# Two chained cross-attentions and their feed-forwards: new orders on every engine, and the last two batches' second-attention stacks kept in the first attention's buffers

## What is computed

```python
x = x + xattn0(layernorm(x), ctx, ctx)      # 16 heads of 16, 128 queries x 128 keys, causal mask
x = x + ffn0(layernorm(x), ...)             # base matrix + 8 LoRA experts, two picked by a router
x = x + gamma * xattn1(layernorm(x), ctx)   # 8 heads of 16 rows, 256 queries x 256 keys (rows are channels), no mask
x = x + ffn1(x, ...)                        # RMS norm, 8-bit quantised 256->1024, GELU, quantised 1024->256
```

## Time and profile before

| | us |
|---|---|
| median of 3 runs | 407.16 (403.74 to 408.58) |
| the profiled execution | 404.29 |
| its span, first to last instruction | 402.6 |
| outside the span | 1.7 |
| busy: PE / DVE / POOL / ACT | 306.0 / 315.4 / 268.4 / 262.1 |
| mean share of full TensorE clock | 0.919 |

### The profile page before, as it was taken

The page is one execution under the profiler, slowest core; times in us unless marked ns, Lnnn a source line. Parts: engine busy times, 40 slices in busy tenths (PEclk is TensorE's granted clock), DMA queues, the critical chain, the costliest instruction groups (busy, mean ns, idle before and its releaser), DMA issues.

```text
span 402.6 us, 9610 instructions
## 1 busy us (share of the span) xinstructions
PE 306.0 (76%) x2946; PEld 189.5 (47%) x2946; DVE 315.4 (78%) x841; ACT 262.1 (65%) x501; POOL 268.4 (67%) x508
## 2 busy tenths in 40 slices
PE   0156757568889999999987999999768777556784
PEld 0134544435646556556564575665334333334553
DVE  6734447399899688799995998998786467999993
ACT  2313435425769699698686786687455348989993
POOL 5554798777988888979996795655621113677554
PEclk9988667587899999999999999999897689999999
DMA  5677578675686775756775756623451400001111
GB/s 182 184 236 241 136 176 227 164 200 166 164 222 152 210 221 153 220 174 178 219 188 157 221 154 195 133 71 77 95 119 38 95 1 2 0 15 40 42 54 65
DMA packets 73138, 56.21 MB, mean 140 GB/s; under 512 B 5376, under 2 KB 62592, under 8 KB 73088
## 3 DMA queue, kind: packets, MB, share of 16 engines
q1 hardware_dynamic: 69888, 51.67, 47.1%
q10 hardware_dynamic: 3200, 3.93, 3.5%
HBM read 36.45 MB, written 18.87 MB: 137 GB/s over the span
## 4 chain that ended last, share of the span: by engine, by line
PE 24%; DVE 19%; issue 19%; POOL 13%; DMA 13%; SPq 6%; ACT 4%; POOLq 0%; ACTq 0%; DVEq 0%
DMA q<-max_t 7%; DVE max L1833 6%; DMA k_parts<-k_split 4%; PE ps_u L1226 4%; PE ps_st L1195 3%; DVE hq_t L2293 2%; PE ps_s L1180 2%; PE ps_st L1166 2%; SPq L622 2%; PE ps_ff L1296 2%; PE ps_s L1146 2%; SPq L623 2%; POOL p L904 2%; PE ps_s L1150 1%; PE ps_t L1324 1%
## 5 line engine op out<-in xcount | busy, mean ns | idle before, releaser
L1833 DVE TENSOR_REDUCE max<-ps_s 128x2 f32<-128x512 f32 (+1 forms) x192 | 126.9, 680 | 38.5 <-PE ps_s L1180 21.5
L1547 ACT ACTIVATE p<-ps_st 128x512 f32<-128x512 f32 x128 | 71.1, 599 | 20.2 <-PE ps_st L1195 13.7
L1180 PE MATMUL ps_s<-k,q 96*128 96x256 bf16 x256 | 52.0, 288 | 7.5 <-issue 3.2
L904 POOL TENSOR_SCALAR_AFFINE_SELECT p<-p 128x512 f32<-128x512 f32 x64 | 40.0, 637 | 16.6 <-ACT p L1537 16.4
L1195 PE MATMUL ps_st<-q,k 98*128 98x256 bf16 x256 | 47.3, 286 | 3.8 <-ACT p L1547 2.1
L1537 ACT ACTIVATE p<-ps_st 128x512 f32<-128x512 f32 x64 | 35.6, 600 | 21.1 <-PE ps_st L1166 20.7
L1226 PE MATMUL ps_u<-p,v 128*32 128x256 f32 x512 | 39.9, 425 | 6.0 <-POOL v L894 3.6
L1166 PE MATMUL ps_st<-q,k 98*128 98x128 bf16 x256 | 27.1, 250 | 16.8 <-DMA q<-max_t 16.2
L1180 PEld LDWEIGHTS ps_s<-k,q 96*128 96x128 bf16 x256 | 19.4, 100 | 27.3 <-issue 14.2
L1195 PEld LDWEIGHTS ps_st<-q,k 98*128 98x128 bf16 x256 | 21.4, 100 | 20.9 <-issue 7.1
L1166 PEld LDWEIGHTS ps_st<-q,k 98*128 98x128 bf16 x256 | 21.2, 113 | 21.3 <-DMA q<-max_t 13.9
(11 more groups left out here) (144 smaller groups left out, 793.4 us busy)
## 6 DMA issues: line engine op xcount, KB each, us to landing
k_parts<-k_split SPq DMA_DIRECT2D x16, 512.0 KB, 3.8
q<-q_parts SPq DMA_DIRECT2D x32, 256.0 KB, 4.1
k<-k_parts SPq DMA_DIRECT2D x32, 256.0 KB, 3.7
kv_in<-in_kv SPq DMA_DIRECT2D x16, 256.0 KB, 3.8
q_parts<-q_t SPq DMA_DIRECT2D x16, 256.0 KB, 3.7
q<-q_parts SPq DMA_DIRECT2D x32, 128.0 KB, 4.0
k<-k_parts SPq DMA_DIRECT2D x32, 128.0 KB, 3.6
q_parts<-q_split SPq DMA_DIRECT2D x16, 256.0 KB, 2.0
```

The lines of the kernel that those rows point to most:

```text
L904: pool.affine_select(out=kept, in_=kept, compare_op=ALU.is_ge, fill=0.0, base=0, pattern=[[0, G], [1, P]], channel_multiplier=-1).then_inc ...
L1180: last = pe.matmul(out_[:, f * D:(f + 1) * D], q1[0:STK, odd, h * D + f * P:h * D + (f + 1) * P], k1[0:STK, odd, h * D:(h + 1) * D], start ...
L1547: act.activation(p1[:, h, :], ps_st[bank_of(ST_BANKS, f"s1t{h}")][:, :], ACT.Exp, scale=SCALE).then_inc(exp1_done[h], 1)
L1833: dve.tensor_reduce(out_, src, AX.X, ALU.max, negate=True).then_inc(done, 1)
```

## The change

Four parts. (1) The orders of `fill` and `drain` are written anew on every engine, those of `body` on SP, POOL, DVE and in two places on PE (`pv0` of unit 3 goes before unit 0, `pv1(1, 1)` before the last `scores1_t`). (2) In passes 19 and 20 the loads of batches 14 and 15 for the second attention go into `k0` and `q0`, whose last first-attention use is over in pass 17 or 18; they wait for that instead of for batches 12 and 13. (3) `load_v1` has stage 7 instead of 6, `dequant_in` 20 instead of 19. (4) `copy_hid`, `down`, `scale_output`, `add_output` and the store move one stage back, and the program has one pass more. No operation is added or left out.

```diff
-LOAD_V1 = 6
+LOAD_V1 = 7
-DEQUANT_IN = 19
+DEQUANT_IN = 20
-COPY_HID = 27
-DOWN = 28
+COPY_HID = 28
+DOWN = 29
...
-MAX1_UNITS = MAX1, ((6, 5, 2, 0, 1, 3, 7, 4), (5, 6, 2, 0, 1, 3, 7, 4), (5, 6, 2, 0, 1, 3, 7, 4))
+MAX1_UNITS = MAX1, ((5, 6, 2, 0, 1, 3, 7, 4), (5, 6, 2, 0, 1, 3, 7, 4), (5, 6, 2, 0, 1, 3, 7, 4))
...
+def among_last(b, n):
+
+    return isinstance(b, int) and b >= NB - n
...
+        def stacks1(b):
+
+            return (k0, q0) if among_last(b, 2) else (k1, q1)
...
-                if later(b, 2):
+                if among_last(b, 2):
+                    sp.wait_ge(st0_ready[in_turn(S0T_UNITS, b)[-1]], b + 1)
+                    plain(sp)
+                elif later(b, 2):
                     sp.wait_ge(st1_ready[in_turn(S1T_UNITS, b, 2)[-1]], free)
                     plain(sp)
                 sp.wait_ge(k_parts_out, stored_)
                 plain(sp)
-                load_stack(sp, k1, odd, k_parts[b, 1], K_SECOND, k1_landed)
+                load_stack(sp, stacks1(b)[0], odd, k_parts[b, 1], K_SECOND, k1_landed)
...
             def body(t, odd):
                 load_kv(t, odd)
+                store_k(t)
                 rows1(t, odd)
-                store_k(t)
-                load_q0(t, odd)
                 rows0(t, odd)
+                load_v1(t, odd)
                 load_k0(t, odd)
+                load_q0(t, odd)
                 store_q1(t)
-                load_v1(t, odd)
                 load_k1(t, odd)
                 load_q1(t, odd)
                 store_q0(t)
```

More of the change, by code:

```diff
@@ L772, in body @@
                 load_kv(t, odd)
+                store_k(t)
                 rows1(t, odd)
-                store_k(t)
+                rows0(t, odd)
+                load_v1(t, odd)
+                load_k0(t, odd)
                 load_q0(t, odd)
-                rows0(t, odd)
-                load_k0(t, odd)
                 store_q1(t)
-                load_v1(t, odd)
                 load_k1(t, odd)
@@ L784, in drain @@
             def drain(t, odd):
+                load_kv(t, odd)
                 store_k(t)
+                store_q0(t)
                 rows1(t, odd)
+                load_q0(t, odd)
+                load_v1(t, odd)
+                rows0(t, odd)
                 load_k0(t, odd)
-                rows0(t, odd)
-                store_q0(t)
                 store_q1(t)
-                load_kv(t, odd)
-                load_q0(t, odd)
                 load_k1(t, odd)
                 load_q1(t, odd)
-                load_v1(t, odd)
                 store_out(t)
@@ L997, in fill @@
             def fill(t, odd):
+                if t == 2:
+                    rstd0_group(2)
+                q1_mid(t)
                 k_rest_(t, odd)
-                q1_mid(t)
+                q1_low(t)
+                k_mid(t)
                 place_v0(t, odd)
@@ L1339, in fill @@
                 scores1_t(t, odd, 4)
+                scores1_t(t, odd, 6)
+                scores1_t(t, odd, 2)
+                turn_u0(t)
                 scores1(t, odd, 6)
-                turn_u0(t)
                 scores1(t, odd, 0)
                 scores1(t, odd, 2)
+                turn_gated(t)
+                scores1_t(t, odd, 1)
+                turn_back(t)
+                scores0_t(t, odd, 2)
                 scores0_t(t, odd, 1)
-                turn_gated(t)
-                scores1_t(t, odd, 2)
+                pv1(t, 1, 1)
                 scores1(t, odd, 1)
                 pv1(t, 0, 1)
-                scores0_t(t, odd, 2)
-                scores1_t(t, odd, 3)
+                turn_q0(t)
                 scores1(t, odd, 3)
-                pv1(t, 0, 0)
-                turn_q0(t)
+                scores0_t(t, odd, 3)
                 scores1(t, odd, 7)
+                turn_u1(t)
+                lora(t)
                 scores1(t, odd, 4)
                 scores0_t(t, odd, 0)
-                scores0_t(t, odd, 3)
-                scores1_t(t, odd, 0)
-                lora(t)
+                pv1(t, 0, 0)
                 scores0(t, odd, 2)
+                scores0(t, odd, 3)
                 turn_max1(t)
-                scores0(t, odd, 3)
+                pv0(t, odd, 2)
                 turn_xh1(t)
@@ L1423, in body @@
                 scores1_t(t, odd, 5)
-                pv1(t, 1, 1)
             def turn_in(t):
@@ L2123, in fill @@
                 maxima1(t, 7)
-                maxima1(t, 4)
+                if t == 2:
+                    stats0_group(3)
                 if t == 4:
                     stats0_group(4)
+                maxima1(t, 4)
                 split_max1(t)
@@ L2295, in drain @@
             def drain(t, odd):
+                stats3_(t)
+                copy_hid(t)
                 logits_(t)
                 top_(t)
-                stats3_(t)
                 index(t)
-                quant_in(t)
                 gap_(t)
```

255 lines of the change are left out of this document (125 added, 130 removed).

## The result

The changed kernel takes 401.05 us, the median of nine runs (397.99 to 408.75); the kernel before, beside it, 406.67 us. The ratio is 0.9899, 95% interval 0.9856 to 0.9942: 1.0% faster, where 2.4% was forecast. Run once more beside other kernels, unaltered, it gave 0.9832 (0.9773 to 0.9892). The intervals overlap; still, ratios of different sets of runs should be compared to no better than some 0.7 points. The profiled execution took 401.05 us, its span 399.2.

What follows compares the result with a forecast made beforehand. Hand-overs and DRAM transfers bound the fill, busy engines the body. Gains of 6.4 fill, 0 body, 2.1 drain, 0 tail sum to 8.5, giving 395.8 us, median put at 397.2; forecast's own range 391 to 403, whole range 390 to 407.

Steps and rivals of the forecast that it cites:

- the store ahead costs nothing: Body: issuing the K store before the second attention's rows counted at 0; ends 3 us gained, 5 lost.
- The second rival: Body: K store delays the rows PE awaits, 2.2 us in each of eight passes, 17 us, total 413; chance 0.16.
- Start, 1.4: Fill start: first k stack load runs under the q store, so scores begin 1.4 us earlier; ends 0 and 1.4.
- Rows ahead of the loads, 2.9 net: Fill, passes 4 to 6: maxima rows issued earlier save 5.8 us of PE waits, half counted, 2.9; ends 0 and 12.0.
- first rival: Fill: bytes bound it, so the wait moves to the stacks; row terms 0, pass 7 half; median 401.7 us; chance 0.25.
- Statistics out of pass 7, 2.1: Fill, pass 7: moving six statistics on DVE behind the last maxima gains 2.1 us; ends 0 and 2.5.
- Fill together, 6.4: Fill: sum of the start, rows and statistics terms, 1.4 + 2.9 + 2.1 = 6.4 us gained.
- Drain, 2.1: Drain: 2.8 gained, 2.5 lost, 1.8 gained, sum 2.1 us; ends 4.6 gained and 0.7 lost.
- The stacks: Drain: loading batches 14 and 15 into buffers already free removes PE's waits of 1.11 and 1.73 us, 2.8 gained.
- `place_v1` behind `rms_`: Drain, passes 20 to 22: POOL places v later, 0.8 us a pass, together 2.5 us lost.
- The 1.8 us for unit 6's scores: Drain: unit 6's scores before two `pv1` let DVE finish one maximum early, 0.6 in three passes, 1.8 gained.
- Tail, 0 (±1): Tail: one pass more but no instruction more, DVE's 55.5 us stay; counted 0, ends 1 us either way.

Runs made afterwards that it cites:

- e15: Kernel before, with one pair swapped in SP's body queue: K store ahead of the rows of the second attention's maxima; 1.3% slower (5.5 us).
- e9: Changed kernel with one pair swapped back in SP's body queue: rows of the second attention's maxima ahead of the K store; ratio 0.9861.
- e14: Changed kernel with rows of the second attention's maxima ahead of the K store in SP's body queue, and v placed before the drain's small MLP steps; ratio 0.9698.
- e5: Changed kernel with SP's queue in the fill in the order of before; fill 2.0 us longer than the mean of the new ones, total time not given.
- e13: Changed kernel run once more, unaltered, beside other kernels; ratio 0.9832.
- e6: Changed kernel with the fill's last six statistics again ahead of pass 7's first maxima on DVE; pass 7 took 17.0 us, total time not given.
- e11: Kernel before with only the last two batches' second-attention stacks moved into the first attention's k and q; ratio 0.9904.
- e16: Kernel before with only the new fill and the moved stacks of the last two batches; body, drain and tail in the old orders; ratio 0.9739.
- e7: Changed kernel with the last two batches' second-attention stacks back in k1 and q1; 1.3% more time, drain 3.0 us longer than the mean of its relatives.
- e10: Changed kernel with POOL's placing of v ahead of the three small MLP steps in the drain, as before; ratio 0.9887.
- e12: New fill, drain and stacks with the body of before on all engines, and v placed ahead of the small steps in the drain; ratio 0.9799.
- e8: Changed kernel with the hidden copy, down product, scaling and output addition at their old stages, one pass less; ratio a point above 0.9899.
- e1: Changed kernel with the nine body passes in the order of before on every engine; ratio 0.9889.
- e4: Changed kernel with fill and body in the order of before, only drain orders, tail stages and last two batches' stacks new; measured time not given.

## Why the prediction was wrong in size

**The step that failed is the body's term, "the store ahead costs nothing".** It was read from the nearest row, pass 16 in the earlier trace rows, and that row was not near. The store and the rows go out together there, 0.45 us apart, as in every pass of e15. `k_low` is not the difference: it ends 1.0 us before the split in pass 16 and 1.1 before it in e15's pass 15, where PE waits 1.57 us. But batch 16 doesn't exist, so no 256 KB kv load stands ahead of the two, and PE is in the order of `drain`; which of these made the row mislead was not tried. (The row called pass 10 beside it is of pass 11 by the count of the stages.) The second rival named the mechanism rightly, its point of decision not, since pass 16 meets it without a wait, and it priced it at 2.2 us a pass, 17 in all. Alone it costs 1.3 a pass, 12 us in the profile (e15). Within the changed kernel's new orders less is left, 148.2 - 143.8 = 4.4 us (its mean body against that of e9 and e14), of which 1.9 lie in the unsteady pass 15. The ends, 3 gained and 5 lost, held; the value inside them was wrong. Against the old orders the body lost 148.2 - 144.9 = 3.3.

**Start, 1.4: right.** The turn of pass 2 stands at 23.6 instead of 25.0, and the first scores begin at 18.76, where 18.8 was forecast.

**Rows ahead of the loads, 2.9 net: half of it came.** 11.2 of the 12.0 us of waits went, twice what I counted, and 6 to 8.5 us of new ones came at the q stack, in pass 3 too, which I had not looked at: that pass grew by 2.6 us or more, from 10.8 to 13.4. Passes 3 to 6 together take 58.2 us in the mean of the four old fills and 56.8 in that of the twelve new ones, some 1.5 less. So the first rival was half right. The Trainium skill's rule that the DMA engines alternate between queue rows ("DMA: Bandwidth & Descriptors", "Queues, rings and completion order") would have kept pass 6's wait of 5.36 if the weights in ACT's queue were its cause. The wait is gone in the changed kernel, but that settles nothing: in e5, with the old queue, it is 1.23 us although the rows took 4.3 and 5.8 us to land, nearly as before (5.2 and 6.6), since PE comes to them later, behind 2.98 us for `u`. With the rows first they took 4.1 and 4.6 in the changed kernel and 1.7 and 2.0 in e13, the same code. What part the weights have in this stays open.

**Statistics out of pass 7, 2.1: too much.** Pass 7 is 1.2 us shorter in the mean, 17.4 to 16.2, and with the statistics back in their place it is 17.0 (e6): 0.8 us. The first rival had half of the term. PE waits for the gated products instead, 1.80 us.

**Fill together, 6.4.** By profiles 4.2 (100.8 - 96.6). By times 1.65 points, some 6.7 us, from e11 to e16; but these are of different sets, and their median times differ by 3.6 us only (401.05 and 397.45). The times don't decide.

**Drain, 2.1: right as a sum, by two errors.** The stacks are worth 4.8 in two passes and not 2.8 (e11; 3.0 within the changed kernel, e7), because of the clock. `place_v1` behind `rms_` costs some 2.3, near the 2.5 that was forecast: 61.6 to 59.2 (e10) and 59.5 (e14). That is luck: PE's waits only changed their names, and the gain was a pass at full clock. The 1.8 us for unit 6's scores were not seen: with v placed first, the new drain takes what the old one takes with the stacks, 59.5 (in e12 61.2). That place was not tried alone.

**Tail, 0 (±1): wrong, 2.0 lost.** Two stretches of the last 60.2 us, before and after (columns as above):

```profile
342.30:350.30 8.00, 3.80 (x31) 2.32 (x32) 7.89 (x26) 7.77 (x14) 5.62 (x16) 1.00 0.00 0
...
366.30:370.30 4.00, 2.81 (x28) 1.80 (x25) 3.96 (x11) 3.81 (x8) 2.97 (x9) 1.00 0.10 35
```

```profile
338.90:347.20 8.30, 6.93 (x35) 3.72 (x36) 8.23 (x25) 7.60 (x13) 5.43 (x14) 0.59 0.00 0
...
363.20:367.20 4.00, 4.00 (x23) 2.51 (x23) 3.14 (x9) 2.74 (x6) 2.96 (x7) 0.60 0.04 14
```

PE is busy 6.93 us for 35 records where it was 3.80 for 31: at a granted 0.59 it works most of that time at 1.2 GHz. Every kernel with the new drain shows such stretches, and so do e11 and e16 with the old one; the three tails at a mean clock of 0.98 take 77.3 to 77.4 us, those at 0.91 to 0.93 take 78.0 to 78.5, the others up to 80.2. In the pass behind the last split PE waits 1.85 us for v, where it was 1.02, but e9, which waits as long there, has a tail of 78.1. DVE is busy 55.1 of the last 64.5 us, so that the slower PE costs little. With the old stages the second stretch is absent and nothing is gained (e8); it is absent with the new stages too in e9, e10 and e14. What makes the clock fall there is not shown. The forecast's 0 took for granted that the tail would stay at its clock of 1.00.

**The sum.** By the parts of the profiles, in means, 4.2 - 3.3 + 2.7 - 2.1 = 1.5 us were gained where 8.5 were forecast: the body lacks 3.3 of it, the fill 2.2 and the tail 2.1, and the drain gave 0.6 more. In times the new fill and the stacks have 2.6 points (e16), about as much as the whole forecast, and the changed kernel in the same set has 1.7: the new orders of body, drain and tail give back 0.9. So the gain was there, and a loss beside it that I had seen and set at nothing. The profiles give less than the times; the profiled execution of before lies 2.4 us below its median, and that difference is not located.

## What to carry to other kernels

Where two things wait in one in-order queue, ask of each pass which is ready first, and take a row as evidence only if the same things are ready in the same order there; a row from the edge of a loop, where a load is missing, is not the body. When a wait for a small transfer goes, write down which transfer is now last in that queue and what waits for it, and read the granted clock of a pass beside its waits: a wait that lies in a stretch at the lower level lengthens it, and a pass can get shorter with as much waiting as before. A large reordering is best timed in pieces: here the stacks of two batches alone had as much as the whole change, and one swapped pair in one queue made the whole of the body's loss.

## What was not expected of the hardware

- The clock's share: two waits of 2.8 us in sum went, and PE's busy time for the same matmuls fell by another 2.0 (e11). In e10 PE's waits stayed as they were in sum, and its busy time in the drain fell by 1.7.
- Pass 15, the second of the code's loop over passes 14 and 15, took 17.6 us before and 18.4 after, but 16.0 in e1, 16.2 in e4 and 18.7 in e11, which all have the orders of before there. What it is stays open.
- The fill of one and the same code ended at 94.5 us in one profile and 97.0 in another: a single wait for the q stack in pass 5, 0.56 us or 2.93, makes most of it.
